# First-chunk down products moved ahead of the low-rank session, in a fused adapter-FFN kernel on one core

## What is computed

```
gate = x @ Wg.T + lora(x, A_gate[i], B_gate[i])        # 512 -> 1376, rank 16, per sequence
up   = x @ Wu.T + lora(x, A_up[i], B_up[i])
act  = silu(gate) * up
down = act @ Wd.T + lora(act, A_down[i], B_down[i])    # 1376 -> 512
x1   = x + down @ sign(W).T + bias0
out  = x1 + lora1(x1, B[j], A[j]) + x1 @ (W1 + sum of 8 adapters).T + bias   # what the kernel folds
```

## Time and profile before

| | |
|---|---|
| median of 3 runs | 875.0 us (874.68 to 875.05) |
| the profiled execution, its own time | 874.75 us |
| its span, first to last instruction | 872.9 us |
| outside the span | 1.85 us |
| busy TensorE matmul, weight load, VectorE, ScalarE | 99%, 82%, 60%, 27% |
| from one small session to the next, in the loop | 23.16 us into an odd step, 27.27 us into an even one |

### The profile page before, as it was taken

One profiled execution on the slowest core, in us unless ns is written; L12 is line 12 of the kernel. 1 busy time (PEld: TensorE's weight loads), 2 busy tenths in 40 slices (PEclk: granted clock), 3 DMA queues, 4 the chain that ended last, 5 costly groups with the idle time before them and its releaser, 6 DMA issues.

```text
span 872.9 us, 21554 instructions
## 1 busy us (share of the span) xinstructions
PE 867.7 (99%) x7474; PEld 714.2 (82%) x7474; DVE 523.2 (60%) x1204; ACT 231.5 (27%) x460; POOL 86.8 (10%) x122
## 2 busy tenths in 40 slices
PE   9999999999999999999999999999999999999998
PEld 6888888888888888888888888888888888888885
DVE  5797556655555566556556665655656565656654
ACT  4953212222222122212222231212122222212210
POOL 0232000000010000100000000000000000000011
PEclk9999999999999999999999999999999999999999
DMA  9967788685877767587876757688675768868563
GB/s 347 408 229 267 228 253 262 195 268 163 257 250 237 249 219 239 180 257 227 256 247 227 245 178 248 208 268 256 223 238 184 245 198 264 265 217 266 190 173 89
DMA packets 159771, 205.60 MB, mean 236 GB/s; under 512 B 56064, under 2 KB 121600, under 8 KB 152064
## 3 DMA queue, kind: packets, MB, share of 16 engines
q1 hardware_dynamic: 101536, 117.14, 43.1%
q10 hardware_dynamic: 56096, 80.76, 27.8%
q0 software_dynamic: 2112, 7.34, 2.2%
HBM read 158.76 MB, written 15.20 MB: 199 GB/s over the span
## 4 chain that ended last, share of the span: by engine, by line
PE 99%; DVE 1%; ACT 0%; issue 0%; DVEq 0%
PE gu_ps L1125 56%; PE y_ps L1230 27%; PE out_ps L1252 3%; PE gu_ps L1340 3%; PE out_ps L1303 2%; PE gu_ps L1331 1%; PE out_ps L1239 1%; PE y_ps L1125 1%; PE out_ps L1125 1%; PE gu_ps L1230 1%; PE out_ps L1260 1%; PE gu_ps L1424 0%; DVE a_lo L817 0%; PE gu_ps L1380 0%; DVE weff_raw L1032 0%; PE y_ps L1307 0%
## 5 line engine op out<-in xcount | busy, mean ns | idle before, releaser
L1230 PE MATMUL y_ps<-down_sb,actT_sb 128*128 128x512 f32 x1023 | 241.5, 393 | 0.0
L1230 PEld LDWEIGHTS y_ps<-down_sb,actT_sb 128*128 128x128 f32 x1023 | 189.6, 188 | 60.3 <-issue 21.4
L1125 PE MATMUL gu_ps<-wg_sb,xT_sb 128*128 128x432 f32 x768 | 164.0, 362 | 0.5 <-DVE act_all L835 0.5
L1125 PE MATMUL gu_ps<-wu_sb,xT_sb 128*128 128x432 f32 x768 | 160.8, 358 | 0.0
L1125 PEld LDWEIGHTS gu_ps<-wu_sb,xT_sb 128*128 128x128 f32 x768 | 144.5, 188 | 8.3
L1125 PEld LDWEIGHTS gu_ps<-wg_sb,xT_sb 128*128 128x128 f32 x768 | 141.7, 188 | 11.6 <-DVE xT_sb L817 1.4
L591 ACT CAST actT_sb<-landed 128x512 fp32r<-128x512 f32 (+1 forms) x96 | 51.1, 585 | 162.1 <-DMA landed<-act_all 89.4
L537 POOL TENSOR_TENSOR b_two<-b_raw,const_sb 128x128 f32<-128x128 f32 x62 | 24.2, 411 | 685.4 <-DMA b_raw<-in_b1tab 685.4
L1125 PE MATMUL gu_ps<-slot,s_sb 128*128 128x512 f32 x270 | 66.8, 392 | 0.0
L839 DVE STREAM_TRANSPOSE act_all<-act_all 128x512 f32<-128x512 f32 (+1 forms) x96 | 64.1, 668 | 3.3
L591 ACT COPY ad_two<-a_raw 128x352 f32<-128x352 f32 x64 | 28.0, 485 | 126.2 <-PE out_ps L1252 125.5
(11 more groups left out here) (173 smaller groups left out, 929.9 us busy)
## 6 DMA issues: line engine op xcount, KB each, us to landing
slot<-t_table ACTq DMA_DIRECT2D x59, 1024.0 KB, 8.0
b_rows<-in_btab SPq DMA_DIRECT2D x128, 236.0 KB, 3.2
a_raw<-in_atab SPq DMA_DIRECT2D x128, 152.0 KB, 8.0
landed<-act_all SPq DMA_DIRECT2D x132, 64.0 KB, 4.7
xT_raw<-in_xT SPq DMA_DIRECT2D x32, 256.0 KB, 2.6
x_in<-in_x SPq DMA_DIRECT2D x32, 256.0 KB, 10.3
landed<-act_all ACTq DMA_DIRECT2D x124, 64.0 KB, 4.7
out_x<-out_sb SPq DMA_DIRECT2D x31, 256.0 KB, 8.3
```

Of the source, the lines that this page charges most:

```text
L1125: last = nc.tensor.matmul(o, w, m, start=start and n == 0, stop=stop and n == len(terms) - 1, skip_group_check=not check)
L1230: last = nc.tensor.matmul(to[:], actT_sb[:, ACTT_SLOT[c] + n, a, :], down_sb[:, blk, b, :], start=begin and (c, n) == (0, 0) and (a, b) == ...
```

## The change

Three things are moved. `down(prev, 0)` (nine matmuls) now runs right after `up(g, 2)`, ahead of the waits of the low-rank session. It opens the sum in `y_ps` (`begin=True`), and `down_rows` in the session no longer does. The wait on `x1_done`, which guards `y_ps`, goes with it. The down products of chunks 1 and 2 stay behind the session.

```
-            def down_rows(n, to=y_ps, begin=True):
+            def down_rows(n, to=y_ps):
                 return nc.tensor.matmul(to[pair(n), :], lhs_sb[group(3), pair(n)], cs_rows[group(3), n, :],
-                                        start=begin, stop=False, skip_group_check=True)
+                                        start=False, stop=False, skip_group_check=True)
...
                     pe.wait_ge(L["td_ready"], g)
                     pe.wait_ge(L["sbd_in"], 16 * GB * g)
-                    after(pe, L["x1_done"], prev)
...
                 gate(g, 2)
                 up(g, 2)
+                if prev is not None:
+                    after(pe, L["x1_done"], prev)
+                    down(prev, 0, begin=True).then_inc(L["y_mm"], 1)
                 lora_ready(g, j, parity, prev, pp)
                 first_rows(prev, pp)
                 second_rows()
                 if prev is not None:
-                    for c in range(NC):
+                    for c in range(1, NC):
                         down(prev, c).then_inc(L["y_mm"], 1)
...
                 for n in range(PAIRS):
-                    last = down_rows(n, y_end, False)
+                    last = down_rows(n, y_end)
```

## The result

The median is 876.08 us (20 runs, 875.8 to 877.54), against 874.96 us for the kernel before (20 runs): the ratio is 1.0014, interval 1.0008 to 1.002. The forecast was 876.4. The change makes the kernel about 1.1 us slower. That is less than the 1.75 us that the prediction took for what can be told, but the interval of these 20 runs leaves out 1.

What follows compares the result with a forecast made beforehand. The prediction took TensorE to be the bound in every step. Its terms, 0 + 0 + 0.3 + 1.1 = 1.4 us on the profiled 874.75, gave 876.15, and 0.25 more for the median gave 876.4; range 875.0 to 878.5.

Steps and rivals of the forecast that it cites:

- Nine matmuls ahead of the session: On TensorE, the moved matmuls' 2.08 us are spent ahead of the session instead of behind it: 0.
- The switch into the session: On TensorE, the session follows a 512-column matmul instead of a 432-column one: 0, with 0.9 us kept both ways.
- VectorE's chain shifts by 1.82 us in the loop: Odd to even step: low parts of s1 and s2 come 1.82 us later, within p6's 2.70 us of slack: 0.
- The partial copy and p3: Odd to even step: the shifted copy and following splits end about 411.0, p3's load comes at 411.89: 0.
- Step 3 into 4: Slower sends there leave p6's load 1.59 us, less than the 1.82 shift: 0.3 us, once.
- x1's landing, even to odd: x1's shifted landing at 436.0 precedes the next step's small session at 436.75, 0.7 us left: 0.
- The end: Tile 31's chunk 0 split is late: 1.52 us of new standing minus 0.48 of old, taken as 1.1 us.
- full shift: Rival: landing and ScalarE's queue get in each other's way in `finish`, the end shifts by 2.08, 877.4 us; chance 0.10.
- Faster: Rival: the session's weight loads start earlier because inputs are older, 867.7 or 873.7 us; chance 0.05.

Runs made afterwards that it cites:

- e8: The changed kernel with twelve down matmuls ahead of the session in place of nine, old order in step 31: 875.62 us, ratio 1.0007.
- e9: The changed kernel with fifteen down matmuls ahead of the session in place of nine, old order in step 31: 881.83 us, ratio 1.0078.
- e6: The changed kernel with 21 down matmuls (chunks 0 and 1) ahead of the session, old order in step 31: 921.19 us, ratio 1.0534.
- e4: The changed kernel with ScalarE's two x1 sends ahead of its two loads of table rows in the last step: 876.52 us, ratio 1.0019.
- e11: The changed kernel as it is, run a third time: 876.47 us, ratio 1.0018 to the kernel before.
- e1: The changed kernel as it is, run again for a second profile: 876.88 us, ratio 1.0022 to the kernel before.
- e3: The kernel before with the change in step 31 alone: 876.06 us, ratio 1.0012.
- e7: The kernel before with tile 31's splits and ScalarE's x1 sends earlier, three chunk 2 matmuls ahead of the narrow session of `finish`: 874.54 us, ratio 0.9995.
- e5: The changed kernel with three down matmuls ahead of the session in place of nine, in all steps: 874.83 us, ratio 1.0002.
- e10: The kernel of e7 with three down matmuls ahead of the session in steps 1 to 30: 874.43 us, ratio 0.9992 to the kernel before.

## Why the prediction was right, step by step

**Nine matmuls ahead of the session: 0.** Right. Two groups of 2.15 and 5.58 us and a session of 1.77, where there were 7.63 and 1.77.

**The switch into the session: 0, at most 0.9 either way.** The switch costs the same 0.09 us behind a 432-column and a 512-column matmul, by the groups' distances. The idle time of the load grew from 0.29 to 0.35 us, about as foretold (0.33); 0.04 of that is only the longer matmul, and the distances show none of it as a cost. That the page's idle time of the weight load is no cost on TensorE's path is what to see in it.

**VectorE's chain shifts by 1.82 us in the loop; p6 has 0.88 left: 0.** Right: 1.79 in step 15, with 0.64 left there and 0.93 in the median passage, and e8, e9 and e6 put the edge near the slack of 2.70 us. What can be spent is 0.1 us less, since a load that waits starts 0.07 to 0.13 us behind the low part.

**The partial copy and p3: 0.** Right: the copy ends at 409.11 and p3's load comes at 412.26, neither waited for.

**Step 3 into 4: 0.3, once.** This did not occur. The distance is 27.28 like the others, since the eight sends that had taken 6.17 us there took 5.41, and the low part ends 0.77 us ahead of p6's load. One slow case in one execution was taken for a property of that step.

**x1's landing, even to odd: 0.** Right, and the even to odd distances stay at 23.17 us with twelve ahead. With fifteen two of them are 0.1 and 0.3 longer; in e6 all are.

**The end: 1.1.** Right in size and place (1.51 new, 0.48 gone, 1.06 in e4 and e11), for executions without the second wait. The sentence that failed is "x1's DMAs, the small session of `finish` and the last outputs follow with the same shift". They do not. The kernel before, the two queues' sends of x1:

```profile
857.42 1.19 SPq L350 DMA_DIRECT2D x_landed<-x_turn  x2
...
857.42 1.47 ACTq L350 DMA_DIRECT2D x_landed<-x_turn  x2
```

Both started 857.42 - 840.16 = 17.26 us behind the small session of step 31. SyncE's now start 858.96 - 840.76 = 18.20 behind it, 0.94 later, ScalarE's 859.68 - 840.76 = 18.92, 1.66 later, because they stand behind the split of chunk 1, which is late, and the two loads of `load_sbd`. That brings them to within 0.1 to 0.2 us of the load of x_in, and in some executions behind it. This is the place of the rival "full shift", with the queue that it names, and its 2.08 is measured as 2.2 in the first profile, 2.3 in e1. It had 0.10. Of the three profiles of the changed kernel two have it, so the rival was underrated, though the median of the first 20 runs does not show it.

**The loop's 0.4 us** was in no term, though within the bounds of the switch's. It is 0.013 us a step, spread over all steps (27.28 and 23.17 in place of 27.27 and 23.16). All six profiles with nine ahead in the loop have it (756.69 to 756.81, against 756.38 to 756.50 in before, e3 and e7). The starts of the single matmuls in the traces show where it lies. Behind a session or a change of shape the next down matmuls are 0.224 to 0.236 us apart before they settle at 0.227. In the kernel before that is nine distances in a step; with nine ahead it is six in each of the two runs of down products, and their excess over 0.227 adds up to 0.01 us more. What makes the distances uneven is open. A second start alone does not cost it: e5 starts twice as well, has only six such distances, and its loop is 0.2 us shorter than before. Nor does TensorE's order alone decide it. In e10, which has e5's order in the loop, and in e7, which has that of before, ten or so distances behind the session are up to 0.240 us in the even steps. In e10 these are the whole of its 0.6 us over e5 (23.19 in place of 23.15).

**Faster** is refuted. The session takes 1.77 us though it starts 2.06 us later and its inputs are older by that, and the load stands 10.6 us ahead of 30 of them, 0.35 each, and not less than before.
The Trainium skill's "TensorE: Matmul & The Clock Gate", the mechanism of Part 3, was weighed against this: by its second half, loads overlap only where the row groups differ, nothing can be won here, and the trace agrees, by these 0.35 us.

The sum of what was found is 1.06 + 0.4 = 1.5 us for an execution without the second wait, against 1.4 forecast and 1.1 to 1.9 between the medians of the three sets of runs. That forecast and result agree so well is in part luck: 0.3 that did not occur stood for 0.4 that was not foreseen. Why the three medians lie 0.8 us apart is not shown.

## What to carry to other kernels

Where work moves ahead of a point on the engine that bounds the kernel, nothing is paid in the middle as long as what that point releases has slack; the slack can be read beforehand, and it was right to a few tenths here, with an edge as sharp as nine, twelve and fifteen matmuls. The price is at the end, where the moved work was the last cover of a tile that no later step hides. There each queue has to be shifted by itself: a DMA behind a late instruction shifts by more than its neighbours, and what it then meets on the other queues can cost as much as the wait that one saw.

## What the runs showed that was not expected

- A send of 64 KB of x1 at the end lands in 2.0 to 2.4 us if it is issued ahead of SyncE's load of 256 KB, and in 3.2 to 3.3 us if ScalarE issues it 0.1 us behind that load (first profile, e1, e3). Which of the two comes first is settled by 0.1 to 0.2 us, so the end of the same program took 33.8 us in one profile and 34.9 to 35.0 in two.
- The profiled loop with three matmuls ahead took 756.19 us in e5 and 756.83 in e10, whose edits lie outside it, while the changed kernel repeats to 0.1 (756.79, 756.69, 756.79). Each is one execution, and e10's is the slowest of its eleven, 0.97 us above the median, so its loop need not be typical.
- The weight load's wait for a low part is put down to "issue" however long it is (9.4 us in e9, 29.3 us in e6). The matmul's waits name the releaser, but for 4 of the passages in e9 (0.8 us in all) and 13 in e6 (19.7 us).
